# Sums of x on TensorE for five chunks instead of eight, over four banks with x's product first, and a new order of all engines' instructions in the last joint steps

## The reference, cut to what matters

```python
x = L0_attn_x                      # [2, 2048, 256]
xn = _layernorm(x, axis=-1)
s = _L0_attn_ref(xn, ...)          # delta-rule attention, 4 heads, dk 128, dv 64
g = _silu(_L0_ffn_ref(xn, ...))    # 8 experts, argmax of the router chooses one per token
x = x + s * g
return x
...
pred = jnp.einsum('bhk,bhkv->bhv', k_t, S)      # the recurrence, one token at a time
delta = (v_t - pred) * b_t[..., None]
S = S + k_t[..., :, None] * delta[..., None, :]
o_t = jnp.einsum('bhk,bhkv->bhv', q_t, S)
...
o = o * jax.lax.rsqrt(jnp.mean(o * o, axis=-1, keepdims=True) + EPS) * norm_w
o = o * (g * jax.nn.sigmoid(g))
return o.reshape(b, n, H * DV) @ Wo
...
h = jnp.square(jax.nn.relu(jnp.einsum('btd,edh->ebth', x, expert_fc)))
out_e = jnp.einsum('ebth,edh->ebtd', h, expert_proj)
```

## Time and profile before

| what | value |
|---|---|
| median of 3 runs | 796.69 us (796.59 to 797.21) |
| the profiled execution: its time | 798.03 us |
| its span, first to last instruction | 796.2 us |
| TensorE busy | 769.3 us, 97% |
| DVE, ACT, POOL busy | 524.7, 349.5, 388.5 us |
| DMA: bytes and mean rate | 116.25 MB, 146 GB/s |

### The profile page before, as it was taken

One profiled execution on the slowest core, in us unless ns is written; L12 is line 12 of the kernel. 1 busy time (PEld: TensorE's weight loads), 2 busy tenths in 40 slices (PEclk: granted clock), 3 DMA queues, 4 the chain that ended last, 5 costly groups with the idle time before them and its releaser, 6 DMA issues.

```text
span 796.2 us, 22202 instructions
## 1 busy us (share of the span) xinstructions
PE 769.3 (97%) x9002; PEld 650.8 (82%) x9002; DVE 524.7 (66%) x1151; ACT 349.5 (44%) x762; POOL 388.5 (49%) x407
## 2 busy tenths in 40 slices
PE   6969999999999999999999999999999999999977
PEld 5957888888888888888888888888787887879854
DVE  6686565665755557465575655776777777677786
ACT  4823434444344444444444343444444444435432
POOL 3725373544625456263552635446464646445341
PEclk9999999999999999999999999999999999999999
DMA  9608634533344343432534335314042333323075
GB/s 303 214 2 326 231 126 171 188 114 132 126 184 165 114 155 130 182 139 114 182 129 167 129 114 204 149 34 181 34 152 88 128 113 121 128 107 114 9 245 199
DMA packets 37748, 116.25 MB, mean 146 GB/s; under 512 B 3664, under 2 KB 24400, under 8 KB 27664
## 3 DMA queue, kind: packets, MB, share of 16 engines
q1 hardware_dynamic: 33904, 104.62, 35.8%
q0 software_dynamic: 3744, 10.23, 3.9%
HBM read 101.33 MB, written 13.50 MB: 144 GB/s over the span
## 4 chain that ended last, share of the span: by engine, by line
PE 84%; DVE 6%; POOL 4%; issue 4%; DMA 1%; another core or an unknown queue 0%; ACT 0%; DVEq 0%; POOLq 0%; SPq 0%
PE bank L504 18%; PE bank L515 16%; PE bank L548 6%; PE bank L580 6%; PE bank L533 6%; PE bank L480 4%; PE bank L478 4%; PE bank L479 3%; PE bank L722 2%; PE bank L629 2%; PE bank L620 2%; PE bank L638 2%; PE bank L435 2%; PE bank L560 2%; POOL XTl L2392 1%
## 5 line engine op out<-in xcount | busy, mean ns | idle before, releaser
L515 PE MATMUL bank<-wts,hT 128*128 128x256 f32 x624 | 171.2, 393 | 0.0
L504 PE MATMUL bank<-xsT,wts 128*128 128x128 f32 x1248 | 166.2, 281 | 0.1
L504 PEld LDWEIGHTS bank<-xsT,wts 128*128 128x128 f32 x1248 | 150.8, 192 | 11.7 <-issue 11.7
L2392 POOL TENSOR_TENSOR XTl<-f_t,XTh 128x512 f16<-128x512 f32 x32 | 39.6, 1241 | 151.6 <-DVE XTh L1695 151.5
L1755 DVE TENSOR_TENSOR Pm<-bank,lvl_mask 128x256 f16<-128x256 f32 x180 | 68.2, 419 | 65.9 <-PE bank L620 62.5
L515 PEld LDWEIGHTS bank<-wts,hT 128*128 128x128 f32 x624 | 105.3, 191 | 7.3
L1766 DVE TENSOR_TENSOR M<-bank,M 128x256 f16<-128x256 f32 x180 | 68.9, 419 | 51.0 <-PE bank L629 50.6
L1201 ACT CAST Z<-bank 128x256 f16<-128x256 f32 x180 | 59.4, 376 | 91.3 <-PE bank L638 91.2
L1146 ACT ACTIVATE hT<-bank 128x512 f32<-128x512 f32 x78 | 46.7, 599 | 50.9 <-PE bank L504 50.9
L580 PE MATMUL bank<-wvg_sb,xT 128*128 128x512 f32 x128 | 63.4, 618 | 0.0
L548 PE MATMUL bank<-xT,wq_sb 128*128 128x128 f32 x512 | 63.1, 276 | 0.0
(11 more groups left out here) (247 smaller groups left out, 1948.0 us busy)
## 6 DMA issues: line engine op xcount, KB each, us to landing
wts<-in_fc SPq DMA_DIRECT2D x39, 1024.0 KB
wts<-in_pj SPq DMA_DIRECT2D x39, 1024.0 KB
wts<-in_x SPq DMA_DIRECT2D x10, 512.0 KB, 7.6
wts<-y_d SPq DMA_DIRECT2D x4, 1024.0 KB, 9.5
out_x<-wts SPq DMA_DIRECT2D x16, 256.0 KB, 2.3
xn_d<-wts SPq DMA_DIRECT2D x3, 1024.0 KB, 4.4
x_first<-in_x SPq DMA_DIRECT2D x4, 512.0 KB, 17.4
wts<-in_x SPq DMA_DIRECT2D x4, 256.0 KB, 3.4
```

The source lines that it names most:

```text
L504: ins = pe.matmul(psum[bank[n]][:, (c % 4) * P:(c % 4 + 1) * P], fcw[r][:, k, c * P:(c + 1) * P], xsT[:, k, :], start=(k == 0), stop=(k == ...
L515: ins = pe.matmul(psum[bank[0]][:, 0:D], hT[:, c, :], pjw[r][:, c, :], start=(c == 0), stop=(c == HC - 1))
L2392: pool.tensor_tensor(h4(XT[1][a % 2], b), h4(f32_t, b), h4(XT[0][a % 2], b), ALU.subtract).then_inc(Xl_ok[b], 1)
```

## The change

`ON_PE` names five chunks instead of eight, so DVE adds x for the chunks 9, 10 and 11 too. The sums take four banks in turn (6 or 7, 7 or 6, 0 and 1: the expert banks, and the two that the solve of chunks up to 14 used), and each sum is split in two: `begin_sum(c)` multiplies x, which has long been there, and `add_y(c)` adds y. In the new list for TensorE the first stand at other places than the second. The lists of all four engines are written anew from the step of chunk 13 on.

```diff
-        ON_PE = [0, 2, 4, 6, 8, 9, 10, 11]
+        ON_PE = [0, 2, 4, 6, 8]
+
+        SUM_BANK = [*H_BANK, 0, 1]
...
         def sum_bank(c):
-            return psum[H_BANK[added(c) % 2]][:].rearrange("p (b d) -> p b d", b=B)
+            return psum[SUM_BANK[(added(c) - 1) % len(SUM_BANK)]][:].rearrange("p (b d) -> p b d", b=B)
...
-                def add_x(c):
+                def begin_sum(c):
+
                     n = added(c)
-                    if n == 1:
+                    if n <= 2:
                         At(pe, NT - 1).on(y_ok)
-                    if n > 2:
-                        pe.wait_ge(out_act, n - 2)
+                    elif n <= len(SUM_BANK):
+                        At(pe, NCH - 2).on(*dZf_ok)
+                    else:
+                        pe.wait_ge(out_act, n - len(SUM_BANK))
                     pe.wait_ge(xf_in[c // (NCH // 2)], 16 * B * GROUPS // 2)
                     pe.matmul(sum_bank(c), ident[:], x_of(c), start=True, stop=False)
+
+                def add_y(c):
                     pe.wait_ge(ys_ok, c + 1)
                     pe.matmul(sum_bank(c), ident[:], chunk_of(c), start=False, stop=True).then_inc(sum_ok, 1)
```

And POOL's list from gate_y(36) on, whose diff is:

```diff
+                    gate_y(36)
                     ImM_(14, 0)
+                    send_y(35)
                     ImM_(14, 1)
-                    send_y(35)
-                    gate_y(36)
+                    gate_y(37)
                     P_l(15, 0)
-                    gate_y(37)
                     send_y(36)
                     send_y(37)
                     gate_y(38)
                     send_y(38)
```

More of the change, by code:

```diff
@@ L1037, in tail @@
+                    L(14, 3)
+                    experts(4)
+                    Dm(14, 3)
+                    L(15, 0)
+                    VG(15, 0)
+                    Dm(15, 0)
                     T(14, 3)
-                    wo(13)
+                    experts(2)
                     L(14, 4)
-                    experts(4)
+                    T(15, 0)
+                    experts(2)
                     Dm(14, 4)
-                    M0(15)
-                    experts(2)
-                    L(15, 0)
+                    KS(14)
@@ L1077, in tail @@
                     ogT_(14)
-                    L(15, 5)
-                    Dm(15, 5)
+                    T(15, 5)
                     wo(14)
-                    T(15, 5)
+                    F(15)
                     KS(15)
-                    F(15)
-                    add_x(0)
+                    add_y(0)
+                    begin_sum(4)
                     Zc(15)
                     U(15)
-                    add_x(2)
-                    add_x(4)
+                    add_y(2)
@@ L1089, in tail @@
                     O(15)
-                    add_x(6)
-                    add_x(8)
-                    add_x(9)
-                    add_x(10)
+                    begin_sum(6)
+                    begin_sum(8)
+                    add_y(4)
+                    add_y(6)
+                    add_y(8)
                     ogT_(15)
-                    add_x(11)
                     wo(15)
@@ L2226, in tail @@
                     Pm_(15, 5, 1)
+                    S32_(14)
+                    dM(15, 5, 0)
+                    S_h(14)
+                    dM(15, 5, 1)
+                    S_l(14)
+                    weigh(0)
+                    v(15, 1)
+                    weigh(1)
                     gate_(15, 1)
-                    dM(15, 5, 0)
-                    weigh(0)
-                    weigh(1)
-                    dM(15, 5, 1)
                     weigh(2)
+                    add_x(1)
@@ L2233, in tail @@
                     weigh(3)
+                    Fr_(15, 0)
+                    Fr_(15, 1)
                     R32(15)
-                    Fr_(15, 0)
+                    weigh(4)
                     R_h(15)
-                    Fr_(15, 1)
-                    weigh(4)
+                    weigh(5)
                     R_l(15)
-                    add_x(1)
-                    weigh(5)
+                    add_x(3)
+                    weigh(6)
                     U_h(15)
-                    weigh(6)
+                    weigh(7)
@@ L2244, in tail @@
                     U_l(15)
-                    weigh(7)
-                    add_x(3)
+                    add_x(5)
                     weigh(8)
-                    add_x(5)
+                    add_x(7)
+                    weigh(9)
                     oss_(15)
-                    weigh(9)
+                    weigh(10)
+                    add_x(9)
                     og_(15)
-                    weigh(10)
-                    add_x(7)
                     weigh(11)
+                    add_x(10)
@@ L2255, in tail @@
                     weigh(12)
+                    add_x(11)
                     weigh(13)
```

378 lines of the change are left out of this document (186 added, 192 removed).

## The result

The changed kernel took **800.18 us** (median of six runs, 797.43 to 802.51) against 796.62 us for the one before (795.82 to 797.21), ratio 1.0043, 95% interval 1.0032 to 1.0054. It is slower by 0.4% where 0.3% faster was forecast, and outside the forecast's range of 793.4 to 795.1 us and the one of 8 in 10, 792.8 to 797.0. Its runs spread over 5 us, those of before over 1.4. The profiled execution took 799.88 us with a span of 798.0.

The account below looks back on a forecast made before the run. TensorE, 97% busy, bounds it up to the tail; then state chain, y's way and stores. Stores behind chunk 4 end the span at 793.9 against 796.2, 2.3 us less: 794.4 us by the median, range 793.4 to 795.1 (8 in 10: 792.8 to 797.0).

Parts of the forecast that it names:

- (1): TensorE's reordered joint steps 13 to 15: no new waits, most of one 0.5 us wait gone, e at 755.6 against 756.54.
- e: The moment the last expert product gives way on TensorE's timeline: 756.54 us before, forecast 755.6.
- (7): DVE's 27 operations on y: span 793.0, covered by the stores; each POOL operation can hold DVE once.
- (2): y's way through POOL: gate_y(38) at e + 1.6 to 1.9, first product of y on DVE at 766.7.
- (3): DVE from the first product of y to the low half of R(15): 8.4 us, ending 775.1, 0.5 later than before.
- (4): O(15) finds TensorE free, goes at 778.3 and ends at 779.7 against 780.57: 0.9 us won.
- (5): Chunk 4's copy out at 783.1, later than before; twelve stores behind it run without a break and end the span at 793.9.
- (6): The data chain after O(15), through og, ogT and wo, is no longer last: it would end at 792.9.
- C: Rival: levels of steps 13 to 15 wait in turn, six or seven places of 0.6 us, slower by 0.2%; chance 0.16.
- B: Rival: the new order gives the gain back by new TensorE waits or later y; span 795 to 797; chance 0.25.
- D: Rival: idle TensorE drops to half clock at the end, ogT and wo take 2.2 us more, median 795.6; chance 0.03.
- A: Rival: stores keep up or e comes 0.7 us earlier, so (6) and (7) end it, 793.4 us median; chance 0.14.

Follow-up runs that it names:

- e9: The changed kernel with POOL (GpSimd) waiting for R_l(14) ahead of gate_y(37), a pause in its train of operations; ratio to before 1.0015.
- e1: The changed kernel with R_l(14) moved on DVE behind the sums dM(15,2) that T(15,2) needs and both Fr_(14); ratio to before 0.9997.
- e4: The kernel before, in its old order, with only the new sums (five chunks on TensorE, four banks, x first); ratio to before 1.0053.
- e5: e4 with one wait more: DVE waits for POOL's og(15) ahead of weigh(11); ratio to before 0.9978.
- e6: e5 with chunk 4's sum done ahead of O(15) and its copy ahead of osq(15) on ACT; ratio to before 0.9974.
- e10: Control: the kernel before with only DVE's wait for og(15) ahead of weigh(11); ratio to before 0.9999.
- e11: e6 with ten added 128x512 products, result overwritten, on TensorE ahead of ogT_(15); ratio to before 0.9966.
- e7: The changed kernel's new order of all engines with before's sums (eight chunks on TensorE, two banks); ratio to before 1.0091.
- e2: The changed kernel with P_l(15,0) moved behind send_y(38) on POOL; ratio to before 1.0004.
- e3: The changed kernel with nine added 128x512 products, result overwritten, on TensorE ahead of T(15,2); ratio to before 1.0017.

## Why the prediction was wrong, by its steps

- **(1) failed, by the sentence "I find no product that must wait".** The step looked for a product between each pair of hand-overs on TensorE and found it. It didn't look at what DVE's operation ahead of the sum costs beside what POOL does in the new order. R_l(14) cost 3.15 us more than its 0.69, T(15,2) waited 2.43 and e lost 1.25 more by the half clock. 2.43 + 1.25 is 3.7; e was 3.6 late. From mark to e, e9 takes 3.0 us of this away with a single pause, and e1 3.9, all of it. T(14,2) waited 0.82 us as well.
- **In (1) the forecast's 755.6 would have been luck even with nothing held.** The step left the 0.7 us wait of L629 in. It is not the order's: before and e4 have it, behind a wait of DVE of 2.6 us at 688 us that the profile marks remote; e5, e6, e10 and e11, with the same order there, don't, and are 1.07 us shorter from mark to e. No kernel with the new order has it either. Against e10 (139.49 us from mark to e) the step's own gain of 0.97 would put e at 138.5, and e1 has 139.9: the new order without the hold is 0.4 us later than the old one, not 1.0 earlier. The waits of M0 went, as forecast (0.94 us in e10), and T(14,2) took 0.82 of that back; some 0.8 us of the difference no row shows as a wait, and their cause stays open.
- **(7) failed in its rule, "each POOL operation can hold DVE once"**, with 0.96 us as the most. The earlier trace rows show no hold longer than that. One instruction was held through three of POOL's (3.84 us), and in the other direction one of POOL's through ten of DVE's (6.87 us). The Trainium skill (SBUF — State Buffer, "Who interferes with whom") has the second to issue wait until the first is done; the runs agree with who is held (two SBUF inputs against a POOL operation that reads SBUF; the subtraction of q with one input in PSUM never) and not with the order or with how long, since R_l's row starts ahead of all three POOL operations that it outlasted. In the changed kernel's end, though, the rule fits. POOL has a train of three there too, and each of its operations held one product of y, 1.43 us at most, and let it in before the next:

```profile
768.64 1.60 POOL L2423 TENSOR_TENSOR ImM<-ident,wk_sb 128x512 f32<-128x512 f16 x1
770.21 1.60 POOL L2409 TENSOR_TENSOR PTl<-f_t,PTh 128x512 f16<-128x512 f32 x1
771.77 1.60 POOL L2423 TENSOR_TENSOR ImM<-ident,wk_sb 128x512 f32<-128x512 f16 x1
```

  So a train without a pause can hold the other engine to its end, and need not. The 793.0 of the step was never tested in the changed kernel, for the stores covered it.
- **(2)** was off by 0.9 us to the good: the first product of y came 10.2 us after e, not 11.1. The step had POOL's list as the last thing ahead of gate_y(38), at e + 1.6 to 1.9. It came at e + 1.1, as in before, after POOL had waited 4.04 us for the sigmoid that ACT makes of the last tile; with e late, the list was not in the way. In e1, where R_l(14) holds up nothing, POOL had no wait there and gate_y(38) came at e + 1.2.

```profile
760.26 0.72 POOL L2376 TENSOR_TENSOR y_sb<-y_sb,y_sg 128x256 f32<-128x256 f32 x1 [4.04 <-ACT y_sg L1176]
```

- **(3)** was too short: 9.7 us from there to the end of R_l(15), not 8.4. Three products of y ran beside POOL, not two (1.43, 1.31, 1.31 us); R_l(15) ended at e + 19.9 against a forecast of e + 19.5.
- **(4)** O(15) started at e + 23.0, forecast e + 22.7, and waited for U_l alone.
- **(5) was right**: the stores end it. Chunk 4 at e + 27.8, forecast e + 27.5, and from there 11.0 us, forecast 10.85. From e to the end 38.84, forecast 38.3.
- **(6)** was covered, as it said; the last product of y started at 793.08.
- **Rivals.** The outcome lies on C's side, but hardly by C: not six or seven places of 0.6 us, but two, of 0.82 and 2.43 us, and the half clock. (C's price for ten places is added up wrongly: 794.4 + 6.0 is 800.4, not 798.2; and B's span of 795 to 797 is 795.5 to 797.5 by the median.) D's mechanism came, at 754 and not at the end. A's state, in which DVE and not chunk 4 sets the end, is that of e11.

Of the 3.6 us between the two medians, then, as a rough account from single profiled executions: the new sums are a gain of 2.1 us (e5 against e10, from e to the end), the new order costs 1.9 us in front of U(15), and the hold with the half clock 3.7, together 3.5. The parts are not independent: from the mark to the end the changed kernel is 2.4 us longer than before and 3.6 longer than e10. Nor does the account explain e7, whose median is 0.9% above before's with the same order.

**What stays open.** Why DVE got in between ImM and the gate product in e2 and e3 and not in the changed kernel and e7, whose R_l(14) stood alike against POOL (0.33 to 0.35 us ahead of ImM in all of them), and why in the changed kernel's end it did at every operation. Why e7's and the changed kernel's other runs are as slow as 807 and 802.5 us, since only one execution of each has a profile; that a hold of og as in e4 strikes in some is likely, not shown.

## What to carry to other kernels

Before putting a VectorE operation with two SBUF inputs, or a GpSimd one, in front of something that the bottleneck waits for, look at what the other engine does in that stretch: not one operation of it may count but, in the worst case seen here, the whole train up to its next pause. Place the waited-for sum ahead of it, or give the train a pause; a semaphore wait of 0.6 us bought 2 us here. But look at the profile for the hold itself: a spread of the runs that has grown from 1.4 to 5 us is a hint and no more, for e4, with the longest hold, spread over 1.2 us, and e1, where nobody waited for the held instruction, over 3.6.

## What the runs showed of the hardware that was not expected

- A wait of 2.43 us brought the granted clock to 0.50 for 2.8 us in the changed kernel (1.25 us more up to e) and left it at 1.00 in e7, at the same place after the same wait. Idle times of 2.4 us have a price that is drawn. The Trainium skill (TensorE: Matmul & The Clock Gate, "What's actually happening") has an idle TensorE fall to 1.2 GHz; both of its levels show here, in e4's wo as 3.78 against 2.0 us.
- With ten products whose result nobody reads the clock stayed at 1.00 in e11, where e6 had 0.50, and from e to the end it took 37.36 us against 37.72. That is one execution of each, and e7 shows that a wait doesn't always lower the clock.
- DVE's copies of fp16 within SBUF are lengthened beside POOL too: 0.28 to 1.98 us for the same 128x512 copy (L1746) in the changed kernel.
- Before's own runs on a chip fall in two groups, about 796.3 and 797.2 us, as wide apart as the 1.07 us by which profiled executions with and without the remote wait at 688 us differ. That the two are the same thing is not shown.
